# Setup of a fused convolution and attention kernel: another engine scales the weights, the order of the setup steps and of the first image's tiles is changed

## The reference

```python
# layer 0
x = x + conv_block(_gn(x), ...)
#   t = silu(bn(conv1x1(x, cv1_w)));  ys = [t[:, :256], t[:, 256:]]
#   for i in 0, 1:
#       z = silu(bn(conv3x3(ys[-1], m_cv1_w[i])))
#       z = attention(z, m_qkv_w[i], m_rw[i], m_rh[i])     # 4 heads of 64
#       z = silu(bn(conv1x1(z, m_cv2_w[i])));  ys.append(ys[-1] + z)
#   return silu(bn(conv1x1(concat(ys), cv2_w)))
# layer 1
x = x + grouped_1x1(_gn(x), conv, S, T)
#   s, t = argmax of softmax(S), softmax(T);  w = conv * gains where t[o] == s[i]
#   dense = conv1x1(x * s_gain, w);  return dense[:, p[p]], p = argsort(t)
```

## Time and profile before

| | |
|---|---|
| median of 3 runs | 3157.91 us (3157.25 to 3157.99) |
| time of the profiled execution | 3157.68 us |
| its span, first to last instruction | 3156.0 us |
| PE busy | 2889.9 us (92%) |
| DVE, ACT, POOL busy | 1962.5, 1716.2, 1150.8 us |
| start of the first product of cv1 | 159.66 us |
| mean granted clock | 0.979 |

### The profile page before, as it was taken

One profiled execution on the slowest core, in us unless ns is written; L12 is line 12 of the kernel. 1 busy time (PEld: TensorE's weight loads), 2 busy tenths in 40 slices (PEclk: granted clock), 3 DMA queues, 4 the chain that ended last, 5 costly groups with the idle time before them and its releaser, 6 DMA issues.

```text
span 3156.0 us, 62539 instructions
## 1 busy us (share of the span) xinstructions
PE 2889.9 (92%) x27616; PEld 1582.0 (50%) x27616; DVE 1962.5 (62%) x2612; ACT 1716.2 (54%) x2148; POOL 1150.8 (36%) x818
## 2 busy tenths in 40 slices
PE   2588999999999999989999999999999899999997
PEld 2354454554545545644546545455455444465453
DVE  7756565765667565665657656675656746566464
ACT  1337384373735656464753838356564647538382
POOL 4326161253424442351612524244322526115151
PEclk7789999999999999999999999999999999999998
DMA  5100000201010010100102010110101001010001
GB/s 166 74 28 31 30 13 28 84 2 41 12 64 38 2 41 28 54 32 1 42 28 84 2 40 12 49 52 2 41 25 58 31 1 41 28 58 2 1 9 47
DMA packets 35903, 111.99 MB, mean 35 GB/s; under 512 B 12976, under 2 KB 15024, under 8 KB 32944
## 3 DMA queue, kind: packets, MB, share of 16 engines
q1 hardware_dynamic: 35632, 107.98, 9.5%
HBM read 85.69 MB, written 22.28 MB: 34 GB/s over the span
## 4 chain that ended last, share of the span: by engine, by line
PE 71%; ACT 12%; DVE 10%; issue 4%; POOL 3%; DMA 0%; POOLq 0%; ACTq 0%; DVEq 0%
PE ps_u L836 39%; PE ps_u L1004 11%; PE ps_u L850 8%; PE ps_o L1025 3%; PE ps_u L978 3%; ACT ps_u L1193 3%; DVE row_max L1440 3%; ACT wide L1193 3%; PE ps_o L1026 3%; PE ps_o L1027 2%; POOL y_rest L1581 1%; ACT probs L1197 1%; POOL z L1581 1%; ACT qk L1172 1%; DVE o_nat L1460 1%
## 5 line engine op out<-in xcount | busy, mean ns | idle before, releaser
L1440 DVE TENSOR_REDUCE row_max<-ps_u 128x2 f32<-128x1024 f32 x512 | 619.0, 1222 | 240.6 <-PE ps_u L978 240.5
L1603 POOL TENSOR_TENSOR probs<-wide,probs 128x1024 f16<-128x1024 f32 x256 | 545.2, 2130 | 182.1 <-ACT probs L1197 171.4
L1004 PE MATMUL ps_u<-qk 64*128 64x512 f16 x3072 | 418.8, 378 | 62.4 <-ACT wide L1193 20.4
L1070 ACT ACTIVATE wide<-ps_u,par_t 128x512 f32<-128x512 f32 x224 | 173.8, 776 | 536.5 <-PE ps_u L836 497.3
L1025 PEld LDWEIGHTS ps_o<-v_ext,probs 128*128 128x128 f16 x4096 | 375.0, 96 | 161.5 <-issue 135.8
L1025 PE MATMUL ps_o<-v_ext,probs 128*128 128x65 f16 x4096 | 431.8, 193 | 0.9
L1026 PE MATMUL ps_o<-v_ext,probs 128*128 128x64 f16 x4096 | 429.2, 195 | 0.0
L1027 PE MATMUL ps_o<-v_ext,probs 128*128 128x65 f16 x4096 | 426.6, 191 | 0.0
L836 PE MATMUL ps_u<-y_pad,w_c 128*128 128x512 f16 x1728 | 394.1, 383 | 0.0
L1214 DVE SCALAR_TENSOR_TENSOR wide<-wide 128x512 f32<-128x512 f32 x256 | 176.9, 693 | 335.1 <-ACT wide L1071 311.0
L1026 PEld LDWEIGHTS ps_o<-v_ext,probs 128*128 128x128 f16 x4096 | 380.6, 97 | 6.2
(11 more groups left out here) (213 smaller groups left out, 4410.0 us busy)
## 6 DMA issues: line engine op xcount, KB each, us to landing
w_c<-w_c_dram SPq DMA_DIRECT2D x7, 3072.0 KB, 10.0
w_c<-w_c_dram SPq DMA_DIRECT2D x8, 2304.0 KB, 8.8
xn<-in_x_dram SPq DMA_DIRECT2D x32, 512.0 KB, 6.1
o_nat<-in_x_dram SPq DMA_DIRECT2D x64, 256.0 KB, 2.6
out_dram<-qk SPq DMA_DIRECT2D x32, 512.0 KB, 2.6
w_c_dram<-w_c SPq DMA_DIRECT2D x1, 3072.0 KB, 9.9
qk<-in_L_conv_m_cv_w_dram SPq DMA_DIRECT2D x2, 1152.0 KB, 5.8
probs<-in_L_conv_m_cv_w_dram SPq DMA_DIRECT2D x2, 1152.0 KB, 9.1
```

The lines of the kernel that those rows point to most:

```text
L1004: ins = e.matmul(ps_u[:, use.slot + q, :], lhsT, rhs, start=k == 0, stop=k == 3)
L1440: e.reduce_max(row_max[:, g % 2, :, it, half], ps_u[:, use.slot:use.slot + 2, :], axis=AX.X).then_inc(*dve_max.up(i, b, g, half, it))
L1603: e.tensor_tensor(p_part(s, 1), wide[:, w.slot, :], p_part(s, 0), ALU.subtract).then_inc(*pool_lo.up("p", i, b, s))
```

## The change

The scaling of the weights goes from GpSimd to ScalarE, as a step of its own, `w_apply`, whose place in the list is apart from that of `w_scale`, the maximum. GpSimd keeps the tap sums of the two c3 (0, ...) groups. The group qkv 0 goes ahead of these two groups. The statistics of image 0, its mean, its variance and the root (`gn_stats`, `gn_mean`, `gn_var`) go forward, ahead of the tap sums; `l1_ranks`, `l1_masks` and the four `l1_rows` go one group further back, behind other groups in number; `l1_weights` is cut into four steps, two behind each of the last two groups, and its last part is a step of its own, `l1_unit`, at the end. The maximum of group 1 goes ahead of `l1_keys`. The first image's cv1 computes the tiles with m = 2, 3 first, and the steps of a tile are staggered: in the list, a tile's products stand with the `cv1_out` of the tile before, the `cv1_lo` and `sums` of the one before that, and the `sums_lo` of the one before that.

```diff
GROUPS = [("c3", (1, 0), 1, CH, TAPS), ("c3", (1, 1), 1, CH, TAPS), ("cv1", (0,), CT, C, 1),
-                  ("c3", (0, 0), 1, CH, TAPS), ("c3", (0, 1), 1, CH, TAPS), ("qkv", (0,), 6, CH, 1),
+                  ("qkv", (0,), 6, CH, 1), ("c3", (0, 0), 1, CH, TAPS), ("c3", (0, 1), 1, CH, TAPS),
                   ("qkv", (1,), 6, CH, 1), ("m2", (0,), 2 * NB, CH, 1), ("cv2", (0,), 2, YT * P, 1),
...
         setup_ring = Ring(6)
+
+        def by_plane(g):
+            return GROUPS[g][0] == "c3" and GROUPS[g][1][0] == 0
...
             plan_group_scale(0)
+            plan("w_apply", 0)
+            plan_group_scale(1)
             plan("l1_keys")
-            plan_group_scale(1)
             plan("l1_row", 0)
             for g in range(len(GROUPS)):
                 plan_group_banks(g)
+                if g + 1 < len(GROUPS) and not by_plane(g + 1):
+                    plan("w_apply", g + 1)
+                if g == 1:
+                    plan_gn(0, 0, "gn_var")
                 if g + 2 < len(GROUPS):
                     plan_group_scale(g + 2)
+                    if by_plane(g + 2):
+                        plan("w_apply", g + 2)
                 if g + 3 < len(GROUPS):
                     plan("w_load", g + 3)
-                if g < 2:
-                    plan("l1_row", g + 1)
+                if g == 0:
+                    plan("l1_row", 1)
+                    plan("gn_stats", 0, 0)
+                    plan("l1_row", 2)
+                    o_ring.take()
+                    plan_gn(0, 0, "gn_mean")
                 if g == 1:
-                    plan("l1_ranks")
-                    plan("gn_stats", 0, 0)
-                    plan_gn(0, 0, "gn_mean")
-                if g == 2:
-                    plan_gn(0, 0, "gn_var")
                     for t in range(CT):
                         plan("norm", 0, 0, t, wide_ring.take(("dve_lo", ("norm", 0, 0, t))))
+                if g == 2:
+                    plan("l1_ranks")
+                if g == 3:
                     plan("l1_masks")
-                if 3 <= g < 3 + CT:
-                    plan("l1_rows", g - 3)
-                if g == 4:
+                if 4 <= g < 4 + CT:
+                    plan("l1_rows", g - 4)
+                if g == 5:
                     plan("bn_tables")
-                if g == 7:
-                    plan("l1_weights")
-                if g == 8:
-                    plan("r_operands")
+                if g >= 8:
+                    for c in range(2):
+                        plan("l1_weights", 2 * (g - 8) + c)
+            plan("r_operands")
+            plan("l1_unit")
             plan("bn_factors")
...
         def plan_cv1(i):
-            for m in range(CT):
+            for m in (range(CT) if i else (2, 3, 0, 1)):
                 for n in range(2):
...
-        for step in plan_cv1(0):
-            plan(*step)
-            plan("cv1_out", *step[1:])
-            plan("cv1_lo", *step[1:])
-            if step[2] >= HT:
-                plan_sums(0, 0, step[2] - HT, step[3], step[5])
-                plan_sums_lo(0, 0, step[2] - HT, step[3])
+        first, first_tiles = [], plan_cv1(0)
+        for at in range(2 * CT + 3):
+            if at < 2 * CT:
+                for tile in islice(first_tiles, 1):
+                    first.append(tile[1:])
+                    plan(*tile)
+            for kind, late in (("cv1_out", 1), ("cv1_lo", 2)):
+                if 0 <= at - late < 2 * CT:
+                    plan(kind, *first[at - late])
+            if 2 <= at < 2 + CT:
+                i, m, n, use, w = first[at - 2]
+                plan_sums(0, 0, m - HT, n, w)
+            if 3 <= at < 3 + CT:
+                i, m, n, use, w = first[at - 3]
+                plan_sums_lo(0, 0, m - HT, n)
@@ -856,13 +877,15 @@
-                    once(pool_small, "scaled", g)
+                    if by_plane(g):
+                        once(pool_small, "tap_sums", g)
+                    else:
+                        once(act_cast, "scaled", g)
@@ -1103,11 +1127,19 @@
+                elif kind == "w_apply":
+                    g, = a
+                    e.wait_ge(*dve_small.at("f", g))
+                    name, at, rows, cols, taps = GROUPS[g]
+                    src = stage[g % 3][:, 0:rows * cols * taps].rearrange("p (m n) -> p m n", m=rows)
+                    for m in range(rows):
+                        ins = e.activation(src[:, m, :], src[:, m, :], ACT.Copy, scale=row[:, g % 3, 3, m:m + 1])
+                    ins.then_inc(*act_cast.up("scaled", g))
@@ -1239,12 +1271,12 @@
                     if g >= 3:
-                        e.wait_ge(*pool_small.at("scaled", g - 3))
+                        e.wait_ge(*act_cast.at("scaled", g - 3))
@@ -1519,24 +1551,16 @@
-                elif kind == "w_scale":
+                elif kind == "w_apply":
                     g, = a
-                    if g >= 3:
-                        e.wait_ge(*u_full.at("w", g - 3, len(banks_of(GROUPS[g - 3])) - 1))
-                    e.wait_ge(*dve_small.at("f", g))
...
-                    for m in range(rows):
-                        ins = e.tensor_scalar(src[:, m, :], src[:, m, :], row[:, g % 3, 3, m:m + 1], 0.0, ALU.mult, ALU.add)
-                    if (name, at[0]) == ("c3", 0):
-                        small(ins, "scaled_taps", g)
+                    if by_plane(g):
+                        e.wait_ge(*act_cast.at("scaled", g))
@@ -1663,7 +1687,7 @@
                     if i:
-                        e.wait_ge(*u_full.at("cv1", i - 1, CT - 1, 1))
+                        e.wait_ge(*u_full.at("cv1", i - 1, (CT if i > 1 else HT) - 1, 1))
```

More of the change, by code:

```diff
@@ L883, in tensor @@
                     once(dve_small, "gn_mean", 0, 0)
+                    once(dve_small, "gn_var", 0, 0)
                     if m:
@@ L889, in tensor @@
                 elif kind == "l1_weights":
-                    e.wait_ge(*act_cast.at("one_hot", CT - 1))
-                    e.wait_ge(*dve_small.at("l1_split", CT - 1))
-                    once(dve_small, "gn_var", 0, 0)
-                    for c in range(CT):
-                        for j in range(2):
-                            if c:
-                                e.wait_ge(*act_cast.at("w_l1", c - 1, j))
-                            for t in range(CT):
-                                ins = e.matmul(ps_o[:, j, :], v_split[:, t, j, c * P:(c + 1) * P], one_hot16[:, t, :], start=t == 0, stop=t == CT - 1)
-                            ins.then_inc(*o_full.up("w_l1", c, j))
+                    c, = a
+                    once(act_cast, "one_hot", CT - 1)
+                    once(dve_small, "l1_split", CT - 1)
+                    for j in range(2):
+                        if c:
+                            e.wait_ge(*act_cast.at("w_l1", c - 1, j))
+                        for t in range(CT):
+                            ins = e.matmul(ps_o[:, j, :], v_split[:, t, j, c * P:(c + 1) * P], one_hot16[:, t, :], start=t == 0, stop=t == CT - 1)
+                        ins.then_inc(*o_full.up("w_l1", c, j))
+                elif kind == "l1_unit":
                     e.wait_ge(*act_cast.at("w_l1", CT - 1, 0))
@@ L1086, in scalar @@
                     g, k, bank, use = a
-                    if g == 3 and k == 0:
+                    if by_plane(g) and not by_plane(g - 1) and k == 0:
                         e.wait_ge(*sent_c3.at(1))
@@ L1105, in scalar @@
                     e.activation(v_split[:, m, 0, :], wf, ACT.Copy).then_inc(*act_cast.up("l1_hi", m))
+                elif kind == "w_apply":
[6 more added lines that the diff above has]
+                    ins.then_inc(*act_cast.up("scaled", g))
                 elif kind == "l1_weights":
-                    for c in range(CT):
-                        for j in range(2):
-                            e.wait_ge(*o_full.at("w_l1", c, j))
-                            e.activation(w_l1[:, j, c, :], ps_o[:, j, :], ACT.Copy).then_inc(*act_cast.up("w_l1", c, j))
+                    c, = a
+                    for j in range(2):
+                        e.wait_ge(*o_full.at("w_l1", c, j))
+                        e.activation(w_l1[:, j, c, :], ps_o[:, j, :], ACT.Copy).then_inc(*act_cast.up("w_l1", c, j))
                 elif kind == "setup_end":
@@ L1318, in vector @@
                         e.tensor_scalar(par_y[:, tiles, 1], t[:, 0, tiles], 0.5 * out_scale, None, ALU.mult)
-                elif kind == "l1_weights":
+                elif kind == "l1_unit":
                     e.wait_ge(*o_full.at("l1_unit"))
@@ L1521, in gpsimd @@
                     small(e.iota(iota_k, pattern=[[1, C]], base=0, channel_multiplier=0, allow_small_or_imprecise_dtypes=True), "iota")
-                elif kind == "w_scale":
+                elif kind == "w_apply":
                     g, = a
-                    if g >= 3:
-                        e.wait_ge(*u_full.at("w", g - 3, len(banks_of(GROUPS[g - 3])) - 1))
-                    e.wait_ge(*dve_small.at("f", g))
```

(13 more changed lines are left out.)

2 lines of the change are left out of this document (removed).

## The result

| | before | changed |
|---|---|---|
| median of four runs each, same chip | 3157.90 us | 3135.10 us (3132.88 to 3135.97) |
| ratio | | 0.9927, 95% interval 0.991 to 0.9944 |
| profiled execution, its span | 3157.68, 3156.0 us | 3135.97, 3133.8 us |
| T, start of cv1 | 159.66 us | 152.80 us |
| first products behind the four conv tiles | 220.43 us | 199.35 us |

22.8 us were gained where 24.2 were forecast. (On the second chip on which the changed kernel was measured, the medians lie 25.3 us apart: 3158.60 and 3133.28 us.) The windows between the two points stand against the earlier trace rows. The columns are the same: us, busy time by engine, granted clock, DMA.

The account below looks back on a forecast made before the run. The prediction took the setup to hang on VectorE and its waits, then TensorE with a pause after cv1. Terms -3.5 + 0.5 - 7.7 - 13.5 = -24.2 us from 3157.68 gave 3133.5 us, overall range 3127 to 3143.

Parts of the forecast that it names:

- What bounds the kernel: Setup hangs on VectorE and its waits; nothing is edited behind 220.43 us, so the gain there is the gain at the end.
- Term 1: Setup up to VectorE's read of the first reordered weight rows, before at 99.93 us: -3.5 us.
- term 2: From the first reordered rows to the end of the fourth `l1_rows`, 36.3 us before: +0.5 us.
- term 3: From the fourth `l1_rows` to the first cv1 product, 23.4 us before; one group's copies hide behind column tiles: -7.7 us.
- term 4: From cv1's start to the end of the first convolution tiles; TensorE's 11.16 us pause and cold clock go: -13.5 us.
- the early root "alone is no gain": In the setup, the root comes some 30 us sooner, no gain alone since cv1's products wait for much else.
- The port conflict: Rival in staggered cv1: VectorE stands still for each GpSimd rounding, third map 2 us later; 3134.5 us, chance 0.2.
- The setup gains nothing: Rival: ranks, masks, tap sums and keys stay slow beside GpSimd, term 1 becomes +3, term 3 halves; 3144 us, chance 0.12.
- gains more: Rival: setup ranks at 1.7 us instead of 2.9, masks shorter, serial chain some 5 us earlier; 3128 us, chance 0.13.
- The pause: Rival: TensorE still stands some us at `wino`, the clock falls, half of term 4 is lost; 3140 us, chance 0.04.

Follow-up runs that it names:

- second trace: The changed kernel run again with no edit, on another chip: 3133.28 us.
- masks first: The changed kernel with the masks moved ahead of the maximum of c3 (0, 1), right behind the ranks: 3133.53 us.
- root late: The changed kernel with variance, root and norm of image 0 behind both groups' tap sums: 3148.67 us.
- load ahead: "scale behind copies" with weight loads ahead of SyncE's 3 MB store and three steps behind the batch norm's root one group later: 3128.33 us.
- weights whole: The changed kernel with layer 1's four column tiles and units in one piece behind the last reordered rows: 3143.60 us.
- old cv1: The changed kernel with the first image's cv1 as before (tiles 0 to 3, a tile's steps in one piece): 3152.46 us.
- ScalarE rounds: The changed kernel with the eight roundings of the first cv1 on ScalarE instead of GpSimd: 3135.10 us.
- only cv1: The kernel before with only the new loop over the first image's cv1 tiles, setup untouched: 3140.07 us.
- scale behind copies: "masks first" with ScalarE's scaling of c3 (0, 1) also placed behind the six copies of c3 (0, 0): 3130.29 us.

## Why the prediction was nearly right, step by step

**What bounds the kernel: right.** The images' order gave nothing back, and the two points carry nearly the whole change: 21.1 us at the second point, 22.2 by the spans of the two profiled executions, 21.7 by their times.

**How much of the sum is luck.** Term 1 came 2.7 us short, term 2 was 0.2 better than forecast, term 3 1.4 short and term 4 0.7 better; 1.1 us more came behind the second point, where I had forecast nothing, and the time around the span grew by 0.5. T was forecast at 148.9 and came at 149.60 to 152.80 in the six traces of the list, a spread of 3.2 us, and the list of before gave 159.66 and 162.68. So a miss of 1.6 us in the time is smaller than the spread of T alone. The large terms carry the forecast; that the time met it this closely is luck.

**Term 1 (-3.5, measured -0.8; -2.75 in the second trace).** The order of events was right almost to the end: the factor of group 1 came at 16.1 (15.9), the third diagonals ended at 32.0 (31.3), the norm started at 44.8 (44.3), the ranks ended at 71.2 (70.3), the maximum of c3 (0, 1) was done at 77.5 (76.5). The scaling took 2.21 (2.2). Of the 2.7 us, 1.0 had come up by then. The rest were the last steps of the serial chain: 7.5 us for the tap sums instead of 6.8, since now VectorE writes the masks beside them ("masks first", where it does not, has 6.9), and 6.35 for the reordering instead of 5.64, which is the clock (0.58 in this trace, and 5.23 us at 0.70 in the second). The remark that the early root "alone is no gain" hid how much hangs on it: in "root late", where it stands late with the variance and the norm, F falls 9.5 us behind even the kernel before. The sum had it right only because VectorE's 6.5 us of low parts stood at the right place in it.

**Term 2 (+0.5, measured +0.3).** Right; the wait for cv2's weights was 0.78 us where 0.8 was allowed. By "load ahead" this wait and the one for the batch norm's root are worth 3.8 us of F to R, which neither kernel had collected.

**Term 3 (-7.7, measured -6.3).** The mechanism is shown by "weights whole". The missing 1.4 us are the units: I took 3.7 us, the row at 147.58 has 5.36, at a clock of 0.66. Where they ran at 1.00, R to T was 15.4 us ("old cv1", "ScalarE rounds") against the 15.7 of the forecast; over the six traces it was 15.4 to 17.3.

**Term 4 (-13.5, measured -14.2).** The maps were ready at T + 15.5, 19.1, 23.8 and 26.2 (15, 19, 22.5, 25). TensorE asked for the third at about T + 23.5, and its weight load waited 0.3 us (the waits, 152 to 200 us):

```profile
PEld ps_u L871 <- DVE wino L1428: 0.3, 1, 0.3
```

So the margin was used up but not overrun. In D the two edits inside this term are not additive, which I had not said.

**The port conflict.** It existed and cost nothing in the end, so the rival's price was wrong. Its mechanism was half right: I had VectorE stand still for each rounding, and the longest stop is GpSimd's. GpSimd's timeline of the changed kernel, then VectorE's:

```profile
162.06 1.00 POOL L1616 TENSOR_SCALAR y_rest<-wide 128x512 f16<-128x512 f32 x1 [1.75 <-DVE wide L1246]
...
168.98 4.04 POOL L1616 TENSOR_SCALAR y_rest<-wide 128x512 f16<-128x512 f32 x1 [3.06 <-DVE wide L1246]
```

```profile
162.49 1.07 DVE L1420 TENSOR_TENSOR probs<-wide 128x480 f32<-128x480 f32 x1
```

The same rounding takes 0.62 us alone. VectorE ran seven instructions with two SBUF inputs each without a gap from 168.82 to 172.54, and the rounding ended 0.48 us behind the last of them; the same rounding took 4.04 or 4.05 us in "only cv1", "weights whole" and "root late". At 162.06 and 164.91 it went otherwise: the rounding stood for one such instruction, came in between two and ended after 1.00 us, and VectorE's next, the first of the sums, took 1.07 and 1.06 instead of 0.65. The Trainium skill, "SBUF — State Buffer", section "Who interferes with whom", names this pair: a VectorE instruction with two SBUF inputs and a GpSimd instruction that reads SBUF exclude each other, and the later one is blocked in full. The two cases of 1.00 us agree with that. The one of 4.04 us goes further, since the rounding stood through seven such instructions; why it did not come in between them no run shows. By "ScalarE rounds" the conflict made the third map 1.6 us later (T + 22.2 against T + 23.8), close to the 2 us that the rival took. That it cost nothing is a matter of where the third map would have stood without it: at T + 22.2, so the conflict filled the gap up to TensorE's request and stopped at its edge.

**The other rivals.** "The setup gains nothing" and "gains more" did not occur: the ranks took 11.1 us together, between the two prices. The pause did not stay, and image periods did not change.

## What to carry to other kernels

When a stage hands over to the next, order and stagger belong together: put what the consumer reads first at the front, and interleave the steps of neighbouring items so that no in-order engine waits inside one; in D either half alone brought 2 to 6 us of 13. Before moving a step ahead of an idle time, follow every queue it stands in: three times here a wait was removed and part of the gain was lost behind it, in ScalarE's copies, in steps that met GpSimd's tap sums, in a colder start of TensorE. A single trace is not enough for a short TensorE piece behind idle time; take its cost at both clock levels.

## What the runs showed of the hardware

TensorE's granted clock in the setup differs between executions of the same list: the same 32 small products took 3.68 us (clock 1.00) to 5.36 us (0.66), and T moved by 3 us. I had expected the trace of before to repeat.

Whole executions of one list differ too, and the longer ones have the lower mean clock. On one chip the kernel before took 3157.3 to 3158.1 us at a mean clock of 0.980 to 0.981 in six executions, 3159.8 and 3159.9 at 0.979 in two, and 3162.5 to 3162.9 at 0.978 in three.

GpSimd can be held up by a whole row of VectorE instructions and not only by one: 4.04 us for a rounding of 0.62. The other way round, VectorE's steps on two and six columns took 1.87 us instead of 0.16 and 0.17 beside GpSimd's tap sums of 2.0 us each and ended with them ("scale behind copies"), so a small step can pay all that is left of the instruction it meets; the step between the two took 0.17.
